# A chain of 100,000 plane rotations, worked in groups: the fields of a group made one group ahead, two scalings moved to ScalarE, VectorE's work in another order

## The reference

```python
def step(mat, t):
    i, j, theta = t
    c, s = jnp.cos(theta), jnp.sin(theta)
    ri, rj = mat[i], mat[j]
    mat = mat.at[i].set(c * ri - s * rj)
    mat = mat.at[j].set(s * ri + c * rj)
    return (mat, None)
mat, _ = jax.lax.scan(step, jnp.eye(256), (idx_i, idx_j, rots))
...
x = x + _layernorm(x) @ mat.T + mix(_layernorm(x))
x = x + experts(_layernorm(x))
```

## Time and profile before

| what | value |
|---|---|
| time, median of 3 runs | 1254.36 us (1253.36 to 1254.96) |
| the profiled execution's own time | 1261.33 us |
| its span, first to last instruction | 1259.4 us |
| mean granted TensorE clock in the span | 0.953 of full speed |
| busy: TensorE, VectorE, ScalarE, GpSimd | 1004.9, 781.1, 490.2, 641.3 us |
| from the first `factor` of the first group to that of the last | 220.89 to 586.54 us |

### The profile page before, as it was taken

How to read it: one execution, slowest core, us unless ns; L and a number is a source line. 1 busy time by engine, 2 the same in 40 slices (tenths; PEclk the granted TensorE clock), 3 DMA queues, 4 the chain that set the end, 5 groups by cost and what they waited for, 6 DMA issues and landing times. The chain is left out here.

```text
span 1259.4 us, 26689 instructions
## 1 busy us (share of the span) xinstructions
PE 1004.9 (80%) x6448; PEld 846.8 (67%) x6449; DVE 781.1 (62%) x2619; ACT 490.2 (39%) x1369; POOL 641.3 (51%) x1134
## 2 busy tenths in 40 slices
PE   0779944989999999899898329999999777777775
PEld 0456634777888888788676228888888666666664
DVE  7576544888888888888489723333333455555553
ACT  0224331555555565555245313433334233333321
POOL 1671037666666666666225605666533344444443
PEclk9999976999999999999999659999999899999998
DMA  8100311651100100011134432333321122222221
GB/s 241 31 1 4 78 55 20 189 155 16 24 14 14 27 14 14 23 17 14 14 117 145 141 96 85 107 117 106 97 66 60 59 71 76 75 72 69 75 72 49
DMA packets 64265, 85.64 MB, mean 68 GB/s; under 512 B 17687, under 2 KB 52404, under 8 KB 63982
## 3 DMA queue, kind: packets, MB, share of 16 engines
q1 hardware_dynamic: 45611, 44.89, 12.7%
q0 software_dynamic: 18624, 40.41, 11.4%
HBM read 53.76 MB, written 33.01 MB: 69 GB/s over the span
## 5 line engine op out<-in xcount | busy, mean ns | idle before, releaser
L1706 PE MATMUL banks<-R 128*128 128x128 f32 x1696 | 214.9, 281 | 0.0
L1706 PEld LDWEIGHTS banks<-R 128*128 128x128 f32 x1696 | 204.2, 197 | 0.3
L1716 PE MATMUL banks<-R 128*128 x848 | 202.3, 382 | 0.0
L813 ACT ACTIVATE R<-banks,b1c 128x128 f32<-128x128 f32 x424 | 131.3, 365 | 104.8 <-PE banks L1706 101.3
L1716 PEld LDWEIGHTS banks<-R 128*128 128x128 f32 x848 | 154.7, 192 | 17.0
L581 POOL DMA_INDIRECT send_d<-R,slot_all x98 | 96.8, 988 | 86.2 <-DVE slot_all L1245 59.3
L805 ACT ACTIVATE R<-banks 128x256 f32<-128x256 f32 x106 | 40.7, 384 | 247.4 <-PE banks L1697 230.7
L1587 PE MATMUL banks<-R 128*128 128x128 f32 x768 | 107.5, 283 | 16.2 <-DVE R L1092 8.3
L1697 PE MATMUL banks<-ident,R 128*128 128x128 f32 x212 | 47.0, 305 | 91.7 <-DMA R<-send_d 89.7
L1587 PEld LDWEIGHTS banks<-R 128*128 128x128 f32 x768 | 95.6, 191 | 33.8 <-DVE R L1092 19.3
L1336 DVE COPY R<-R 128x1024 f32 x106 | 76.4, 720 | 60.4 <-issue 39.4
(11 more groups left out here) (319 smaller groups left out, 1957.8 us busy)
## 6 DMA issues: line engine op xcount, KB each, us to landing
R<-send_d SPq DMA_DIRECT2D x106, 131.0 KB
R<-in_L_ffn_W_dram SPq DMA_DIRECT2D x16, 512.0 KB
R<-in_x_dram SPq DMA_DIRECT2D x6, 1024.0 KB, 11.4
R<-in_x_dram SPq DMA_DIRECT2D x12, 512.0 KB
rec_d<-R SPq DMA_DIRECT2D x1, 3125.0 KB
send_d<-zrow SPq DMA_DIRECT2D x18, 131.0 KB, 2.1
send_d<-R,slot_all POOLq DMA_INDIRECT x98
R<-incl_d,R POOLq DMA_INDIRECT x76
```

The lines of the kernel that those rows point to most:

```text
L813: last = nc.scalar.activation(hT[b][:, c, :], bank[2 + 2 * b + c // 2][:, (c % 2) * P:(c % 2 + 1) * P], ACT.Gelu, bias=b1c[:, bass.ds(e, 1 ...
L1706: last = mm(bank[2 + 2 * b + c // 2][:, (c % 2) * P:(c % 2 + 1) * P], w1c[b][:, kb, c * P:(c + 1) * P], xmT[b][:, kb * P:(kb + 1) * P], st ...
L1716: last = mm(bank[6 + b][:, 0:D], hT[b][:, c, :], w2s[:, bass.ds(e, 1), c, :].rearrange("p a h -> p (a h)"), start=(c == 0), stop=(c == H / ...
```

## The change

GpSimd's `fields` writes its six results into a place of its own (`ahead_fld`), and runs one group further ahead: `fields(1)` now stands before the loop, and the body calls `fields(k + 2)` at its end, behind the gathers. It waits for `taken` and `TB_psum` in place of `swapped`. VectorE gets a new step `take_fields`, one copy of 128 x 24 numbers from there to the old place, right behind `swap`; it waits for `flds_ready`.

`other_rows` no longer multiplies: it writes plain one-hot rows in bf16 (`Ot`). ScalarE multiplies both sets of rows with their factors (`scaled`, eight activations of 128 x 256 in four pairs), and `rows_read` becomes one addition of 128 x 1024 numbers, late in the body. VectorE's part 2 steps (`slot_masks` to `mark_latest`) move forward, and TensorE's `spread_targets` moves from behind `better(k, 1)` to before `better(k, 0)`.

```diff
 def fields(k):
     pool.wait_ge(S["recs_in"], k * (16 * G) + 16 * G)
-    at_least(pool, S["swapped"], k)
+    at_least(pool, S["taken"], k)
+    at_least(pool, S["TB_psum"], k)
...
-    nc.gpsimd.tensor_copy(tb16, tgt).then_inc(S["flds_ready"], 1)
+    nc.gpsimd.tensor_copy(tb16, a_tgt).then_inc(S["flds_ready"], 1)
...
 pool.sem_inc(S["B_ready"], 1)
+fields(1)
 with pool.Fori(0, n) as k:
-    fields(k + 1)
     gather_steps(k + 2)
     gather_blocks(k + 3)
+    fields(k + 2)
...
+def scaled(k, which, gs):                                   # ScalarE
+    act.wait_ge(S["Ot_ready" if which else "Rt_ready"], k + 1)
+    if which == 0:
+        act.wait_ge(S["GT_psum"], k * 2 + 2)
+    else:
+        act.wait_ge(S["B_ready"], k + 1)
+    into, ones_, by = ((Bmat, Rt, c_cs), (Both, Ot, c_co))[which]
+    for g in gs:
+        last = nc.scalar.activation(into[:, g, :], ones_[:, g, :], ACT.Copy, scale=by[:, g:g + 1])
+    last.then_inc(S["scaled_rows"], 1)
...
     apply_v(k, 0)                                           # ScalarE's body
     search_in(k + 2, (2, 3))
+    scaled(k, 0, (0, 1))
     better(k, 1)
     search(k + 3, (0, 1))
     apply_v(k, 1)
+    scaled(k, 0, (2, 3))
     better(k, 2)
     search(k + 3, (2, 3))
     apply_v(k, 2)
+    scaled(k, 1, (0, 1))
     better(k, 3)
+    scaled(k, 1, (2, 3))
     apply_v(k, 3)
...
+def take_fields(k):                                         # VectorE
+    dve.wait_ge(S["flds_ready"], k + 1)
+    nc.vector.tensor_copy(fld[:, 0:6, :]..., ahead_fld...).then_inc(S["taken"], 1)
+    dve.wait_ge(S["taken"], k + 1)
...
 def other_rows(k):
     for g in range(G):
-        last = TS(Both[:, g, :], col0[:, :], c_o[:, g:g + 1], c_co[:, g:g + 1], ALU.is_equal, ALU.mult)
+        last = TS(Ot[:, g, :], col0b, c_o[:, g:g + 1], None, ALU.is_equal)
 def rows_read(k):
-    for g in range(G):
-        last = STT(Bmat[:, g, :], Rt[:, g, :], c_cs[:, g:g + 1], Both[:, g, :], ALU.mult, ALU.add)
+    dve.wait_ge(S["scaled_rows"], k * 4 + 4)
+    TT(Bmat[:, :, :], Bmat[:, :, :], Both[:, :, :], ALU.add).then_inc(S["B_ready"], 1)
...
     swap(k)                                                 # VectorE's body
+    take_fields(k1)
+    slot_masks(k1)
     factor(k, 0)
     targets_rows(k)
     other_rows(k)
+    find_hits(k1, (0, 1))
     factor(k, 1)
     apply_m(k, 0)
-    rows_read(k)
+    find_hits(k1, (2, 3))
     factor(k, 2)
-    slot_masks(k1)
-    find_hits(k1, (0, 1))
+    find_latest(k1)
     apply_m(k, 1)
-    find_hits(k1, (2, 3))
     factor(k, 3)
-    find_latest(k1)
+    mark_latest(k1)
     apply_m(k, 2)
-    mark_latest(k1)
     factor(k, 4)
     other_part(k1)
+    rows_read(k)
     apply_m(k, 3)
...
+dve.wait_ge(S["flds_ready"], n + 2)                         # behind the loop
...
     residual(k, 0)                                          # TensorE's body
+    spread_targets(k + 1)
     better(k, 0)
     apply_v(k, 0)
     residual(k, 1)
     apply_m(k, 0)
     better(k, 1)
-    spread_targets(k + 1)
```

More of the change, by code:

```diff
@@ L140, in gnn_layer @@
         fld = chunk(24, G)
+        ahead_fld = chunk(6, G)
+        Ot = chunk(G, D, dt=BF16)
         pos = chunk(2, G)
@@ L274, in gnn_layer @@
                   "mix_psum mix_acc LT_psum o1_psum W_done o2_psum Y_done V_psum V_done M_psum M_done "
-                  "blk_seen rows_in pos_seen recs_in sought_next found_own flds_own flds_ready TB_psum marks_ready Lready B_own B_ready GT_psum GT_done Rt_ready ST_ready Y_ready D_psum D_done "
+                  "blk_seen rows_in pos_seen recs_in sought_next found_own flds_own flds_ready taken Ot_ready scaled_rows TB_psum marks_ready Lready B_own B_ready GT_psum GT_done Rt_ready ST_ready Y_ready D_psum D_done "
                   "reserve ngroups combT_ok comb_pe comb_dve parts_own setup_own wrg_ok x2_psum x2_done "
@@ L306, in bcast_row @@
             return ap.rearrange("(a n) -> a n", a=1).broadcast_to([P, n])
-        sub, v1, v2, v3, lim, isj, sg, twin, dj, tgt, oth, cs, co, csb, cob, single, lastw = [fld[:, i, :] for i in range(17)]
+        tgt, oth, cs, co, lim, single, csb, cob, lastw, sub, v1, v2, v3, isj, sg, twin, dj = [fld[:, i, :] for i in range(17)]
+        a_tgt, a_oth, a_cs, a_co, a_lim, a_single = [ahead_fld[:, i, :] for i in range(6)]
         posA, posB = pos[:, 0, :], pos[:, 1, :]
@@ L542, in fields @@
                 TTp(v1, v1, v3, ALU.mult)
-                TTp(oth, r_j, dj, ALU.subtract)
+                TTp(a_oth, r_j, dj, ALU.subtract)
                 TTp(sg, r_s, sg, ALU.mult)
                 TTp(twin, twin, r_e, ALU.subtract)
[L546 to L551, removed]
+                level(4, TTp(a_tgt, dj, r_i, ALU.add))
+                TSp(a_single, twin, 1.0, None, ALU.add)
+                TTp(a_cs, r_c, v1, ALU.mult)
+                TTp(a_co, sg, v1, ALU.mult)
+                level(5, TSp(a_tgt, a_tgt, -NOROW, None, ALU.add))
+                level(6, TTp(a_tgt, a_tgt, v1, ALU.mult))
                 TSp(slotnum[:, :], slotnum[:, :], float(CAP * G), None, ALU.add)
-                level(7, TSp(tgt, tgt, NOROW, None, ALU.add))
-                nc.gpsimd.tensor_copy(tb16, tgt).then_inc(S["flds_ready"], 1)
+                level(7, TSp(a_tgt, a_tgt, NOROW, None, ALU.add))
+                nc.gpsimd.tensor_copy(tb16, a_tgt).then_inc(S["flds_ready"], 1)
             pool.wait_ge(S["ngroups"], 1)
@@ L1029, in done @@
                 dve.wait_ge(S["dve"], k * PER + (base2 + i))
+            def take_fields(k):
+                dve.wait_ge(S["flds_ready"], k + 1)
+                nc.vector.tensor_copy(fld[:, 0:6, :].rearrange("p a g -> p (a g)"), ahead_fld.rearrange("p a g -> p (a g)"))\
+                    .then_inc(S["taken"], 1)
+                dve.wait_ge(S["taken"], k + 1)
             def slot_masks(k):
-                dve.wait_ge(S["flds_ready"], k + 1)
                 for g in range(G):
@@ L1101, in other_rows @@
                 for g in range(G):
-                    last = TS(Both[:, g, :], col0[:, :], c_o[:, g:g + 1], c_co[:, g:g + 1], ALU.is_equal, ALU.mult)
-                last.then_inc(S["B_own"], 1)
+                    last = TS(Ot[:, g, :], col0b, c_o[:, g:g + 1], None, ALU.is_equal)
+                last.then_inc(S["Ot_ready"], 1)
             def rows_read(k):
-                dve.wait_ge(S["B_own"], k + 1)
-                dve.wait_ge(S["Rt_ready"], k + 1)
-                dve.wait_ge(S["GT_psum"], k * 2 + 2)
-                for g in range(G):
-                    last = STT(Bmat[:, g, :], Rt[:, g, :], c_cs[:, g:g + 1], Both[:, g, :], ALU.mult, ALU.add)
-                last.then_inc(S["B_ready"], 1)
+                dve.wait_ge(S["scaled_rows"], k * 4 + 4)
+                TT(Bmat[:, :, :], Bmat[:, :, :], Both[:, :, :], ALU.add).then_inc(S["B_ready"], 1)
             def apply_m(k, g):
@@ L1125, in kept @@
                 dve.wait_ge(S["D_done"], k + 1)
+            take_fields(0)
             slot_masks(0)
```

2 lines of the change are left out of this document (1 added, 1 removed).

## The result

The changed kernel took **1314.24 us** (median; the kernel before took 1253.86 us on the same chip), a ratio of 1.0476 with an interval of [1.0453, 1.0499]. The prediction was 1318 us, with a range of 1286 to 1328. One of the four timed executions of the changed kernel took 1509.02 us at a mean granted clock of 0.649: the median has it among its four (without it, it is 1312.6 us), the ratio leaves it out. The profiled execution took 1312.6 us with a span of 1310.7, at a mean granted clock of 0.928.

A forecast was written before the change was run, and what follows sets the result against it. TensorE and VectorE, feeding each other in turn, held the loop; the change adds a ring through GpSimd. 7.9 + 15 x 28.2 - 365.65 - 0.8 = +64.5 us on the median of 1254.36 gives 1318 us, range 1286 to 1328.

The forecast's parts named there:

- The ring: Loop: fields taken, masks, first factor, level 0, apply_v, search_in, gather_steps, gather_blocks, fields; 26.9 us a group, 28.2 with slower clock.
- Fields taken to first `factor`: VectorE, head of body: copy 0.15 us, masks 1.13, two waits on itself 0.1; 1.4 us.
- First `factor` to `pos_seen`: From VectorE's first factor through level 0 and apply_v to ScalarE's signal behind search_in: 3.81 us, as before.
- the clock's term: TensorE's better and apply_v at half clock after some 5 us idle: 1.3 us a group, bounds 0 and 1.4.
- The rival in which the clock stays up: The ring holds at 26.9 us a group but TensorE's clock does not fall: +43.5, 1298 us; chance 32%.
- ScalarE to GpSimd: Hand-over from ScalarE's pos_seen to GpSimd's gather_steps: 0.21 us.
- S + B + F: GpSimd's gather_steps (S), gather_blocks (B) and fields (F) in sequence: 21.44 us, lower bound 20.6.
- Start: First body waits for fields(1): first factor at 228.8 instead of 220.89, 7.9 us later.
- The second ring: ScalarE's scalings ahead of blk_seen, for which gather_blocks waits: counted 0, with 0.5 us as the other end.
- the rival's sum: Apparently the case of blk_seen 0.5 us late or records landing late: 28.7 us a group, 1326 us; chance 7%.
- VectorE's savings: One-hot rows 1.37 to 0.86 us, rows_read 1.67 to 1.22, less 0.15 for the copy: about 0.8 us a group.
- the rival that turned them into a faster loop: Loop: fields ready in time, VectorE and TensorE bound a group at 21.6 us: -36, 1218 us; chance 4%.

The follow-up runs named there:

- experiment 3: Changed kernel with take_fields and slot_masks behind apply_m(k, 0), spread_targets before better(k, 1): 1259.47 us, 1.0015; with VectorE's steps in the earlier order: 1257.58 us, 1.0026.
- experiment 5: Unread 0.96 us GpSimd memset between gather_steps and gather_blocks: changed kernel 1331.97 us, kernel before 1274.33 us; behind gather_blocks in the kernel before 1251.16 us.
- experiment 2: Changed kernel with seven unread products of 128 x 256 added in TensorE's pause, four before and three behind spread_targets: 1304.4 us, 1.0353.
- experiment 1: Changed kernel with the second half of search_in moved on ScalarE before better(k, 0): 1323.13 us, 1.0496; its other run has its own line.
- second run of experiment 1: Changed kernel with both halves of search_in before better(k, 0), both searches made early and the scalings moved behind them on ScalarE: 1272.79 us, 1.0116.

## Why the prediction was right, step by step

- **The ring.** As predicted: `take_fields` waits in every group, GpSimd waits before S and not before F. Confirmed from two sides: with the fields taken later the wait and the loss vanish (experiment 3), and a microsecond on GpSimd costs about a microsecond a group (experiment 5). The wait itself is 3.6 us where 4 to 6 were named, and GpSimd's is 7.0 where about 5 was.
- **Fields taken to first `factor`.** 446.86 to 448.34, 1.48 us (predicted 1.4).
- **First `factor` to `pos_seen`.** 448.34 to 453.37 + 0.19, 5.22 us. The part at the full clock was 3.81, so the clock's term is 1.4 (predicted 1.3, of bounds 0 and 1.4); experiment 2 took 1.4 us out of GpSimd's wait. The pause was mis-sized, though: TensorE's work ended 25.4 us after the fields were taken (471.18 + 1.06), not 23.6, so the pause is 3.9 us and not some 5, and the clock fell all the same. The rival in which the clock stays up is refuted: in this order it is at 1.00 throughout a group only with the added products.
- **ScalarE to GpSimd.** 453.56 to 453.84, 0.28 us (predicted 0.21).
- **S + B + F: the term that was mis-sized.** 453.84 to 474.10, 20.26 us, against the 21.44 taken and even the lower bound of 20.6. S was 6.84 (before 7.23), B 7.48 (7.58) and F 5.94 (6.63). F runs where VectorE stands idle. The prediction said so itself, yet held F at its value beside a busy VectorE; it knew F before the loop, 6.67 us, as a row with VectorE mostly idle. That row was misread. VectorE was busy through most of it (198.49 to 204.02), and GpSimd's short instructions beside it took up to 0.44 us in place of 0.20. The term made the sum 1.2 us too long; the other terms were 0.25 us too short between them.
- **Sum.** 1.48 + 5.22 + 0.28 + 20.26 + 0.03 = 27.27 us against 28.2. Over 15 periods with their few longer ones the mean is 27.5, so this term of the sum came out 9.9 us too high, start and end 0.85 too low: +55.5 measured in the loop for +64.5 predicted.
- **Start.** 8.4 us for 7.9: the fields were ready 0.5 us later than before. Executions differ by more than that: the first `factor` begins at 224.2 to 226.4 us in the six other traces with the fields taken at its head, and at 217.5 to 219.4 in the six without.
- **The second ring.** The prediction weighed that `blk_seen` might come late, and counted 0. It was on time by 0.6 us; experiment 1 shows how thin that was. It stands here by luck, not by working: the rival's sum was never followed round its own ring.
- **VectorE's savings.** Busy time as priced: the one-hot rows 0.87 us, the addition 1.23, the copy 0.18, a group 20.3 for 21.04. But the rival that turned them into a faster loop had a second error, in its 21.6 us a group: with no wait left the group takes 24.0 us (experiment 3). The prediction's remark that without the wait a group would be some 2 us shorter is refuted.
- **The time.** 1318 predicted (its sum gives 1318.8) and 1314.24 measured, or 1312.6, lie closer than their terms, and that is luck. The loop was 9 us too high. Against it stands that the sum was moved to the median of before as if both profiled executions stood equally far from their medians: that of before was 7.5 us above, that of after is the middle one of its three.

## What to carry to other kernels

Where a producer moves to the end of a software-pipelined body, follow the waits round through every engine's queue until they close, add that ring up, and hold it against the period; then look for a second ring that enters one step later. What decides is where the result is taken: the same copy goes with a loss of 60 us at the head of the consumer's body and with none behind its second level. Time saved on an engine that waits for another within each step of the body can come back as waiting, however real it is in the page's first line: 0.7 us a group off VectorE bought nothing here (1.0015, 1.0026 and 1.009).

## What the runs showed of the hardware

**GpSimd is held while VectorE runs one long instruction with two SBUF inputs.** The 1.77 us issue in experiment 2 began during VectorE's addition of 128 x 1024 and ended 0.8 us behind it; its neighbours took 0.95. In the changed kernel the copy of 128 x 4 at the head of B (L498), 0.20 us in the kernel before (L495 there), takes 0.61 beside L1080 (460.68 against 460.03 to 461.25). It began during L1080 and ended with it, and so did the 1.03 us copy of experiment 1 (463.50 to 464.53, beside VectorE from 463.27 to 464.49). An instruction of VectorE that is as long but has one SBUF input did not do it: in the kernel before that copy took its 0.20 us at 406.33, in the middle of

```profile
405.67 1.21 DVE L1049 TENSOR_REDUCE R<-R 128x8 f32<-128x1024 f32 x1
```

With VectorE idle, small instructions of F take 0.20 us, and F as a whole 5.9 us against up to 7.6 us in the second run of experiment 1. The Trainium skill, GPSIMD Engine Reference, section Specifications, says that the two engines share SBUF interfaces and that VectorE's instructions with two SBUF inputs contend; the traces agree, and add that in experiment 2 it was worth 1.1 us a group on a path through GpSimd (B at 8.6 us for 7.5).

**A pause of TensorE of 1.97 us, 0.40 us of products and 1.54 us of pause lowered the clock in every group**, where one unbroken pause of 2.63 us did not the earlier trace rows. The fall cost the 12 products behind it 1.4 us. The length of a single pause thus doesn't tell whether the clock falls.
